# A decoder layer on one core: a routed tile's cast from POOL to ACT, and attention scores at full height

## What is computed

```python
def _L0_xattn_ref(Q, K, V, attention_mask, w_q, w_k, w_v, w_o, b_o):   # 32 heads, 8 groups, head size 16
    q = (Q @ w_q.T).reshape(B, S, G, HG, HD)
    k = (K @ w_k.T).reshape(B, S, G, HD)
    v = (V @ w_v.T).reshape(B, S, G, HD)
    scores = jnp.einsum('bnghd,bmgd->bnghm', q, k) / scale
    ...
    attn = jax.nn.softmax(scores, axis=-1)          # causal, and padding masked
    out = jnp.einsum('bnghm,bmgd->bnghd', attn, v).reshape(B, S, D)
    return out @ w_o.T + b_o

def _L0_ffn_ref(x, gate_w, w1, w2, w3, ws1, ws2, ws3):                 # 8 experts, the best 2 of each token
    scores = jax.nn.softmax(xf @ gate_w.T, axis=-1)
    weights, idx = jax.lax.top_k(scores, K)
    ...
    y = jnp.einsum('etd,te->td', eo, comb)
    z = jax.nn.silu(xf @ ws1.T) * (xf @ ws3.T) @ ws2.T
    return (y + z).reshape(shape)
```

## Time and profile before

| | us |
|---|---|
| median of 3 runs | 1658.7 |
| lowest and highest | 1654.16, 1668.66 |
| the profiled execution | 1648.5 |
| its span, first to last instruction | 1646.5 |
| its mean granted TensorE clock | 0.954 of full speed |

### The profile page before, as it was taken

How to read it: one execution, slowest core, us unless ns; L and a number is a source line. 1 busy time by engine, 2 the same in 40 slices (tenths; PEclk the granted TensorE clock), 3 DMA queues, 4 the chain that set the end, 5 groups by cost and what they waited for, 6 DMA issues and landing times. The chain is left out here.

```text
span 1646.5 us, 24434 instructions
## 1 busy us (share of the span) xinstructions
PE 1490.3 (91%) x7850; PEld 1186.2 (72%) x7850; DVE 907.3 (55%) x2208; ACT 695.6 (42%) x1421; POOL 505.0 (31%) x470
## 2 busy tenths in 40 slices
PE   6999899999999999996999999999979977787784
PEld 4888778888888888885677777677657766565563
DVE  3788653333333333345677467557555586666773
ACT  3444411111111111113877677677842224554562
POOL 3555520220210202201111101100211038888984
PEclk9999899999999999998999999999979998888997
DMA  6000030100101101000000000001016414333443
GB/s 230 1 0 0 1 115 0 39 30 10 39 1 38 38 0 39 16 0 30 17 18 17 3 17 18 3 4 40 1 39 268 153 46 89 66 70 71 78 83 51
DMA packets 20391, 73.31 MB, mean 45 GB/s; under 512 B 2288, under 2 KB 3312, under 8 KB 17840
## 3 DMA queue, kind: packets, MB, share of 16 engines
q0 software_dynamic: 10176, 25.17, 7.9%
q1 hardware_dynamic: 10096, 46.66, 7.7%
HBM read 52.69 MB, written 19.14 MB: 44 GB/s over the span
## 5 line engine op out<-in xcount | busy, mean ns | idle before, releaser
L687 PE MATMUL ps<-feat,wsplit 128*128 128x512 f32 x512 | 201.8, 394 | 8.2 <-POOL wsplit L560 2.9
L1609 DVE CUSTOM_DVE_ANT_0 sc<-ps,msk 128x256 f32<-128x256 f32 (+1 forms) x512 | 157.0, 354 | 86.0 <-PE ps L934 78.8
L1236 ACT ACTIVATE sc<-sc,mxs 128x256 f32<-128x256 f32 (+1 forms) x512 | 199.8, 459 | 9.7 <-DVE mxs L1609 9.1
L688 PE MATMUL ps<-feat,wsplit 128*128 128x512 f32 x512 | 200.9, 392 | 0.0
L689 PE MATMUL ps<-feat,wsplit 128*128 128x512 f32 x512 | 200.6, 392 | 0.0
L1112 ACT ACTIVATE sg<-ps 128x512 f32<-128x512 f32 x64 | 38.3, 598 | 379.6 <-PE ps L689 379.6
L1360 DVE TENSOR_TENSOR m_f<-ps,sg 128x512 f32<-128x512 f32 x64 | 44.2, 691 | 256.4 <-ACT sg L1112 256.4
L483 POOL CAST wsplit<-wraw 128x3072 fp32r<-128x3072 f32 x9 | 24.8, 2750 | 427.7 <-PEq L830 395.8
L1242 ACT COPY pt<-ps 128x512 f32<-128x512 f32 x192 | 113.4, 591 | 90.2 <-PE ps L942 88.9
L942 PE MATMUL ps<-ident,sc 128*128 128x128 f32 x768 | 118.4, 277 | 2.9 <-ACT sc L1236 2.5
L687 PEld LDWEIGHTS ps<-feat,wsplit 128*128 128x128 f32 x512 | 97.1, 190 | 31.9 <-issue 11.8
(11 more groups left out here) (263 smaller groups left out, 3428.6 us busy)
## 6 DMA issues: line engine op xcount, KB each, us to landing
wraw<-weights SPq DMA_DIRECT2D x11, 1536.0 KB, 6.6
rawx<-weights SPq DMA_DIRECT2D x8, 1536.0 KB, 12.8
ctx_raw<-ctx_t SPq DMA_DIRECT2D x8, 512.0 KB, 4.5
h_rows<-hd POOLq DMA_DIRECT2D x16, 256.0 KB, 2.6
out<-acc SPq DMA_DIRECT2D x4, 1024.0 KB, 4.3
acc<-x SPq DMA_DIRECT2D x1, 3584.0 KB, 19.5
qkv_raw<-weights SPq DMA_DIRECT2D x6, 512.0 KB, 7.7
msk_i<-mask SPq DMA_DIRECT2D x8, 128.0 KB, 3.4
```

The source lines that it names most:

```text
L687: nc.tensor.matmul(out_, w_hi, m_hi, start=first, stop=False)
L688: nc.tensor.matmul(out_, w_lo, m_hi, start=False, stop=False)
L1236: ins = nc.scalar.activation(cols, cols, ACT.Exp, bias=mxs[:, u % 4, n:n + 1], scale=-1.0)
L1609: ins = nc.vector.tensor_tensor_reduce(sc[:, u % 4, n * w:(n + 1) * w], ps[:, u % 2, n * w:(n + 1) * w], m_in, -0.25, 3e38, ALU.add, ALU.m ...
```

## The change

In attention, k4T becomes block-diagonal. For each pair of groups it has two halves of 256 columns: in the first half rows 0 to 63 hold one group's k and rows 64 to 127 zeros, in the second the reverse. A matmul over all 128 rows with 256 or 512 columns then gives one query row's scores for both groups of a pair. The units are cut anew: a unit has two heads of both groups (first tile) or one head of both (second tile), with as many columns, DVE and ACT instructions as before, and half as many matmuls for scores. The products with v read two places of the transposed probabilities. k4T has one place, not two; ACT copies it in two half-height instructions; its pieces k4Ta and k4Tb come in slots 19 and 1, and some pieces of q move by one or more slots. DVE writes the zeros once.

In the routed stage the cast for the high parts of the down weights goes from POOL's split_down(i+1) to ACT's down_hi(i+1), behind hT_hi_d(i+2) and scale_rows(i-1). POOL's subtraction and DVE's down_lo wait for it there.

```diff
-PIECES = {0: "n10", 2: "kv", 3: "hT0", 4: "k4T0", 5: "hT1", 6: "k4T1", 7: "n11", 8: "q0",
+PIECES = {0: "n10", 1: "k4Tb", 2: "kv", 3: "hT0", 4: "q4T13", 5: "hT1", 7: "n11", 8: "q0",
           9: "n00", 10: "oT0", 11: "oT1", 12: "q4T00", 13: "q4T01", 14: "q4T02", 15: "q4T03", 16: "q1",
-          17: "wo0", 18: "n01", 19: "q4T10", 20: "q4T11", 21: "wo1", 22: "q4T12", 23: "q4T13"}
+          17: "wo0", 18: "n01", 19: "k4Ta", 20: "q4T10", 21: "wo1", 22: "q4T11", 23: "q4T12"}
...
     quad, r = divmod(u, UNITS // 2)
     part, j = divmod(r, 4)
-    return 4 * quad + j, range(4) if part == 0 else range(2 * part - 2, 2 * part), int(part > 0)
+    pair, odd = 2 * quad + j // 2, j % 2
+    if part == 0:
+        return pair, (2 * odd, 2 * odd + 1), 0
+    return pair, (2 * part - 2 + odd,), 1
...
-        k4T = at("k4T", [P, 2, PAIRS, SEQ], F32R)
+        k4T = at("k4T", [P, PAIRS, 2, SEQ], F32R)
...
                 half = UPN + D
-                pool.wait_ge(d["down"], g - 1)
-                nc.gpsimd.tensor_copy(wsplit[:, slot, 0, UPN:SLOT], raw[:, UPN:SLOT]).then_inc(d["down_hi"], 1)
                 pool.wait_ge(d["down_hi"], g - TILES + 1)
...
             def scores(b, u):
-                v, heads, tile = unit_of(u)
+                pair, heads, tile = unit_of(u)
                 after(pe, c["mx"], UNITS * b + u - 1)
-                rows = slice(64 * (v % 2), 64 * (v % 2) + 64)
-                w = P * (tile + 1)
+                w = 2 * P * (tile + 1)
                 for n, i in enumerate(heads):
-                    mm = nc.tensor.matmul(ps[:, u % 2, n * w:(n + 1) * w], q4T[rows, par(b, 0), 4 * (v // 2) + i, tile * P:(tile + 1) * P],
-                                          k4T[rows, par(b, 0), v // 2, 0:w], start=True, stop=True)
+                    mm = nc.tensor.matmul(ps[:, u % 2, n * w:(n + 1) * w], q4T[:, par(b, 0), 4 * pair + i, tile * P:(tile + 1) * P],
+                                          k4T[:, pair, :, 0:P * (tile + 1)], start=True, stop=True)
...
+                    first = PAIRS // 2 * (name == "k4Tb")
+                    for half in range(2):
+                        rows = slice(64 * half, 64 * half + 64)
+                        ins = nc.scalar.copy(k4T[rows, first:first + PAIRS // 2, half, :], bank[rows, :].rearrange("p (k n) -> p k n", k=PAIRS // 2))
+                    ins.then_inc(piece_read[k], 1)
...
+            def down_hi(g, raw):
+                slot = 1 - g % 2
+                act.wait_ge(d["down"], g - 1)
+                nc.scalar.copy(wsplit[:, slot, 0, UPN:SLOT], raw[:, UPN:SLOT]).then_inc(d["down_hi"], 1)
...
                 if i > TILES:
                     scale_rows(i - 1)
+                if TILES <= i + 1 < ALL:
+                    down_hi(i + 1, raw)
...
+            for half in range(2):
+                rows = slice(64 * half, 64 * half + 64)
+                zeros = causal[rows, 0:P].rearrange("p (o n) -> p o n", o=1).broadcast_to([64, PAIRS, P])
+                for t in range(TPB):
+                    nc.vector.tensor_copy(k4T[rows, :, 1 - half, t * P:(t + 1) * P], zeros).then_inc(c["zeros"], 1)
```

More of the change, by code:

```diff
@@ L336, in decoder_layer @@
         c = signals(
-            "c_", wo_hi="the output weights' hi", ctx_hi="the first context's hi", ones="v's columns of ones and zeros",
+            "c_", wo_hi="the output weights' hi", ctx_hi="the first context's hi", ones="v's columns of ones and zeros", zeros="the halves of k4T that stay zero",
             ctx="contexts loaded, by 16", ctx_s="contexts split", mask_i="masks loaded, by 16", pad="masks of padding",
@@ L340, in decoder_layer @@
             h="tiles normalised", hT_ps="tiles of h transposed in PSUM", hT_hi="their hi", kv_ps="batches with k | v in PSUM",
-            kv_hi="their k's hi", k4T_ps="tiles of split k transposed in PSUM", q_ps="tiles of q in PSUM", q_hi="their hi",
+            kv_hi="their k's hi", k4T_ps="halves of the pairs of split k transposed in PSUM", q_ps="tiles of q in PSUM", q_hi="their hi",
             q4="tiles of q split and doubled", q4T_ps="quarter tiles of q4 transposed in PSUM",
@@ L420, in _ @@
             sp.wait_ge(c["mask"], BATCH)
[L421 removed]
+            k, n = piece_turn("k4Tb", BATCH - 1)
             sp.wait_ge(piece_read[k], n + 1)
@@ L875, in piece @@
                 elif name[:3] == "k4T":
[L876 to L880, removed]
+                    if name == "k4Ta":
+                        ready("kv")
+                    for i in range(PAIRS // 2):
+                        p = i + PAIRS // 2 * (name == "k4Tb")
+                        for t in range(TPB):
+                            tr = nc.tensor.transpose(bank[:, (TPB * i + t) * P:(TPB * i + t + 1) * P],
+                                                     k4[:, t, 2 * p:2 * p + 2, :, :].rearrange("t g r d -> t (g r d)"), ident[:, :])
                     tr.then_inc(c["k4T_ps"], 1)
@@ L951, in attend @@
                     after(pe, c["o_raw"], 4 * b + ends - 1)
-                _, heads, tile = unit_of(u)
+                pair, heads, tile = unit_of(u)
                 for m in range(tile + 1):
                     for j in range(4):
[L955 to L958, removed]
+                        first = (u + j // 2 * 2) % PT_PLACES
+                        two = pt[:, first:first + 2, :]
+                        if tile == 0:
+                            p_in = two.rearrange("p s (i g t) -> p g s i t", g=2, t=P)[:, j % 2]
+                        else:
+                            p_in = two.rearrange("p s (g m t) -> p g m s t", g=2, t=P)[:, j % 2, m]
+                        cols = slice(heads[0] * P, (heads[0] + 4 // (tile + 1)) * P)
+                        mm = nc.tensor.matmul(ps[32 * j:32 * j + 32, 4 + tile, cols],
+                                              v32[:, par(b, back), m, 2 * pair + j, :], p_in, start=(m == 0), stop=(m == tile))
                 mm.then_inc(c["O"], 1)
@@ L1002, in _ @@
             parity_now[0] = 0
+            pe.wait_ge(c["zeros"], 2 * TPB)
             pass_c(0, ("in", "own"))
@@ L1600, in maxes @@
             def maxes(b, u, pb):
-                _, heads, tile = unit_of(u)
+                tile = unit_of(u)[2]
                 hold(dve, c["S"], UNITS * b + u + 1, dve_held)
@@ L1605, in maxes @@
                     hold(dve, c["PT_ps"], UNITS * b + u - 3, dve_held)
-                w = P * (tile + 1)
+                count, w = blocks_of(u)
                 m_in = msk[:, pb, 0, :] if tile == 0 else msk[:, pb, 1:3, :].rearrange("p a n -> p (a n)")
-                for n in range(len(heads)):
+                for n in range(count):
                     ins = nc.vector.tensor_tensor_reduce(sc[:, u % 4, n * w:(n + 1) * w], ps[:, u % 2, n * w:(n + 1) * w], m_in, -0.25, 3e38,
@@ L1646, in _ @@
                 if piece_side(name) == "in":
-                    if name == "k4T0":
+                    if name == "hT1":
                         h_c(0, 1)
```

28 lines of the change are left out of this document (16 added, 12 removed).

## The result

| us | before | changed |
|---|---|---|
| median of 4 runs on one chip | 1656.43 | 1714.45 |
| lowest and highest | 1653.8, 1668.66 | 1713.74, 1716.68 |
| span of the profiled execution | 1646.5 | 1712.0 |
| mean granted TensorE clock in it | 0.954 | 0.943 |

The ratio is 1.0338, with a 95% interval of 1.0284 to 1.0391: the change makes the kernel slower by 58 us. The forecast was 1666, the range ended at 1698, and the result lies outside it. The profiles part the difference cleanly. The first gather of the routed stage starts at 1329.24 and not at 1345.3, so all that lies ahead of it is 16 us faster. From there to the end of the span it takes 382.8 us in place of 301.2, which is 81.6 more. -16.1 + 81.6 = 65.5 is the difference of the spans.

The account below looks back on a forecast made before the run. TensorE was taken to bound attention, POOL and what it releases the routed stage. Attention -36, its start +1 and routed +42 gave +7 on the median 1658.7, so 1666 us; own range 1648 to 1677, whole range 1635 to 1698.

Parts of the forecast that it names:

- The mechanism of the routed loss: Routed stage: each gather waits for the one before through ACT's cast, a one-tile loop of 8.3 us instead of 7.12.
- The subtraction, 1.29 us from the earlier trace: Routed loop term: POOL's subtraction after the cast takes 1.29 us.
- Gather to landing, 3.74 from the earlier trace: Routed loop term: gather to landing 3.7 us median, 3.4 to 4.4, in the sum as 3.74 with 0.04 to the transposes.
- The low clock: Routed loop term: transposes after a wait take 1.12 us, not 0.66; half of 0.46 added for some tiles, giving 8.3.
- The forecast of +42: Routed stage: 36 gathers x (8.3 - 7.12) = 42.5 us slower, bounds +28 to +78.
- Rival (2): Routed loop at its upper bound, low clock in every tile and landings at 4.4: -36 + 78, 1701 us; chance 0.13.
- place (a): Attention, slot 5: hT1's transposes already wait for DVE's hTc, so all 1.2 us that slots 3 to 5 save is lost.
- place (b): Attention, unit 12's exponentials: lead 0.68 us, so 1.8 of the 2.46 us that slots 9 to 14 save is lost.
- place (c): Attention, slot 2, waiting for unit 0's maximum: slots 22, 23, 0, 1 save 1.6 us, 0.44 lead returns, 0.9 is lost.
- cost nothing: Attention: with one k4T place the second pairs' transposes wait, sitting in slot 1 and needed in slot 12, at no cost.
- rival (1): Attention gives nearly nothing because waits for DVE and ACT take up the saving: -10 + 42 = +32, 1691 us; chance 0.17.
- A batch of some 53 us instead of 58: Attention, sign expected in the profile after: this batch length, with new TensorE waits at slots 5, 14 and 2.

Follow-up runs that it names:

- the experiments that break the loop: Two edits of the changed kernel: POOL's gather(i+3) ahead of split_down(i+1), 1610.05 us; ACT's down_hi(i+1) ahead of hT_hi_d(i+2), 1601.01 us.
- the kernels with the gather first: GpSimd starts the gather ahead of its subtraction: in the changed kernel 1610.05 us; in the kernel before, ahead of its cast too, 1644.62 us; also in further combinations.
- the exchange: Pieces n10 and k4Tb exchanged between slots 0 and 1, on the attention half of the change with the cast left on GpSimd: 1613.9 us, ratio 0.9753.
- the kernel with the cast ahead: The changed kernel with ACT's down_hi(i+1) ahead of hT_hi_d(i+2) in ACT's queue, POOL's order unchanged: 1601.01 us, ratio 0.9660.

## Why the prediction was wrong

**The mechanism of the routed loss was right.** Gather, transposes, L1276, cast, subtraction, gather is the chain; the tiles, which had followed each other after 6.1 to 8.8 us by turns and at the end evenly after 6.2, now do so after 9.1 to 9.9, nearly all; and the experiments that break the loop give more than the loss back. The sum of its length failed, 8.3 for 9.37, in two terms; a third held:
- **The subtraction, 1.29 us from the earlier trace rows**, takes 1.79. That row was of a late tile, in which VectorE's L1831 only began 0.94 us after it. When the cast is ACT's, VectorE's L1862 and the subtraction are let go by the same instruction and meet. The prediction had this rule before it and set it aside with the words that the new loop has no DVE step in it. It needs none in it, one beside it is enough. The experiment with L1862 put last shows the whole half microsecond. The Trainium skill, "SBUF — State Buffer", "Who interferes with whom", says that a VectorE instruction with two inputs in SBUF contends with a GpSimd one that reads SBUF, and that whoever comes later is blocked; the trace agrees: L1862 ends at 1454.94, 0.63 us after the subtraction's start, and the subtraction is 0.5 us longer. The right size stood in the trace of the kernel before, in every second tile of its first part:

```profile
1464.41 0.69 DVE L1831 TENSOR_TENSOR wsplit<-rawx,wsplit 128x512 fp32r<-128x512 f32 x1
1464.45 1.81 POOL L658 TENSOR_TENSOR wsplit<-rawx,wsplit 128x512 fp32r<-128x512 f32 x1 [0.18 <-POOL wsplit L656]
...
1466.42 1.89 POOL L639 DMA_INDIRECT hg<-h_rows,ids  x1 [0.16 <-issue]
```

- **Gather to landing, 3.74 from the earlier trace rows**, is 4.20. The issue on GpSimd takes 1.81 us on average and 1.43 before, and from its end to the landing it is 2.39 us in both, so all of the growth is in the issue. This size too was there before: behind eleven of the long subtractions the issue took 1.89 us and the landing came after 4.28, in 10 others it was 1.09 and 3.48, in the last 15 1.36 and 3.74; the median of the earlier trace rows mixes them. In the 11, and now in every tile but one, the issue begins while VectorE is in the middle of its first step for the up weights (L1825, now L1856); in the one without it took 1.33 us. That this is the cause wasn't tried apart. Against a simple story speak the kernels with the gather first: their issue takes 1.1 us, and yet they land after 4.2, whether GpSimd's next step follows at once or, as in the changed kernel with that order, 0.77 us later. The cause of this term stays open.
- **The low clock, "half of 0.46 for some tiles"**, was nearly right: 13 of the 39 sets of transposes took 0.99 to 1.12 us, and the rest 0.6 to 0.7. That is 0.15 a tile.

0.50 + 0.46 for the two terms is 0.96 of the 1.07 us by which the sum fell short, and 35 us of the error in 36 tiles. With 1.80 and 4.28, from the tiles of the kernel before that had the new loop's neighbours, the prediction's own sum is 9.23 us, and 9.38 with 0.15 for the clock; 9.37 was measured. The forecast of +42 became +81.6, over its upper bound of +78 too. Rival (2), the loop at 9.3 us, is what happened to the time, but for other reasons than it gave: it wanted landings at 4.4 and the low clock in every tile.

**Attention kept 2.5 us a batch and not 5.1.** The first part of that working holds: units of the second tile went from 1.45 to 1.11-1.13 us (0.33 for 0.35), those of the first from 1.61 to 1.11-1.13 (0.49 for 0.50). In the batch of 53.0 us, slot by slot (starts of the scores, before and after, us saved):

| slots | forecast kept | measured |
|---|---|---|
| 3 to 5, place (a) | 0 | 0.18 |
| 9 to 14, place (b) | 0.66 | 0.31 |
| 22, 23, 0, 1, 2, place (c) | 0.7 | -0.92 |
| 6 to 8 and 15 to 21 | 3.7 | 2.98 |
| sum | 5.1 | 2.55 |

So place (c) is the step that failed, by 1.6 us a batch. It asked when the maximum of unit 0 is out and when the k transposes are needed, and passed over the bank: the prediction says of k4T's new places that they "cost nothing" and gives a lead back for slot 1, but a piece put into slot 1 changes the neighbour of every piece around it. A wait in slot 2 had been named and did come, but that is luck: it was to be for the maximum of unit 0. The rule of the two banks stands in the section on the kernel before. With the exchange, place (c) keeps 0.78, what was forecast, and slots 3 to 5 lose 0.97 where they had kept 0.18, in waits for VectorE: 3.2 us a batch are kept. So the bank is all of the error in (c), and taking it out gives 0.6 of the 2.5 us that a batch fell short; what is left then is VectorE's chain in slots 3 to 5 (1.0), place (b) (0.35) and the last row (0.7). In the last row the slots behind the products with v save 0.13 to 0.17 where I took 0.26. The sum for the stage was 41 less 5; the batches gave 19.4, of which the start of the stage (1.8 us later, the zero halves among it) and the way from the last scores to the first gather (1.6 longer) took back 3.4, so 16. That is within the bounds, and halfway to rival (1), whose mechanism it is: the waits for ACT and DVE went from 5 to some 40 us.

"A batch of some 53 us instead of 58" was met only by name: 58 is a batch with one of the two standstills in or beside it, and they stayed; 55.5 was the number to subtract from. **The sum**: 19 us of the error are attention's (-35 forecast with the start, -16 measured), 39 the routed stage's (+42.5 and +81.6); +7 became +65.5 between the spans. The median missed by 48 only, and that is luck: the prediction took the median 10.2 us over the profiled execution, and in the changed kernel it was 0.7 over.

## What to carry to other kernels

Before a step moves to another queue, write down what it stands behind there and follow that back to whoever waits for the step. If the two meet, the order of the queue is the change, and the load of the engines is not; here two places earlier were worth 113 us. In such a loop take each duration from a row with the same neighbours: what is let go by the same event will run side by side. First ask whether a stage has one pace: a mean or a median over two, and a row picked from the easier one, gave the two sizes that failed here. And check a releaser that the profile names against the distance between the two steps, tile by tile. When a piece enters an alternation of two banks, list the new neighbour of each piece and who empties its bank. And take the saving of a shorter unit only up to the next engine's chain: of the 8 us that a batch's 24 units save where nothing waits (8 x 0.49 + 10 x 0.33 + 6 x 0.15), a third arrived.

## What the runs showed of the hardware

- A subtraction on GpSimd of 128x512, both inputs in SBUF, took 1.29 us when no such step of VectorE had begun ahead of it, and 1.77 to 1.81 with a two-input SBUF step of VectorE started 0.04 to 0.06 us before; VectorE's 128x1024 step took 1.21 alone and 1.97 when started during GpSimd's. One thing doesn't fit: in eight late tiles of the kernel with the cast ahead the subtraction took 1.84 us, and VectorE's step began only 1.15 to 1.4 us after it. GpSimd's cast of 128x1024 took 2.04 to 2.08 us with VectorE's L1825 begun just before, 1.59 with no step of VectorE beside it, and 1.05 right behind a gather's issue; what makes 1.59 into 1.05 isn't shown.
- A step of TensorE from full-height to 64-row matmuls or back cost 0.09 us (0.53 against 0.44 for four transposes), and doing away with it gave what was worked out.
- An indirect gather of 128 rows lands 3.6 to 4.2 us after its issue starts, by kernel. That is 2.4 us after the issue's recorded end where it follows GpSimd's subtraction, and 3.1 where it follows the addition's issue. Adding DMAs that each wait for the one before to land went at one in 5.9 us.
- VectorE stands still for 2.5 to 2.9 us with no releaser but issue in two of eight attention batches, in both kernels and in all ten variants. I did not test what it is; so its cause stays open.
